# An expert stage on one Trainium2 core: every expert for every token, or sorted blocks of token and expert pairs

## The reference, cut to what matters

```python
logits = xf @ Wr + expert_bias                 # 4096 x 8
top_v, top_i = jax.lax.top_k(logits, 2)
probs = jax.nn.softmax(top_v, axis=-1)
rw = zeros_like(logits).at[arange(T)[:, None], top_i].set(probs)
gate = einsum('td,edf->tef', xf, Wg)           # 8 experts, 256 x 128
up = einsum('td,edf->tef', xf, Wu)
h = silu(gate) * up
eo = einsum('tef,efd->ted', h, Wd)             # 128 x 256
out = einsum('te,ted->td', rw, eo)
out = out + silu(xf @ Sg) * (xf @ Su) @ Sd     # the shared expert, 256 wide
x = layernorm(x + out)
```

## Time and profile before

| | us |
|---|---|
| median of 3 runs | 2544.12 (2532.03 to 2554.59) |
| profiled execution, span | 2541.9 |
| expert stage within it | 1048.7 to 1469.3 |

### The profile page before, as it was taken

How to read it: one execution, slowest core, us unless ns; L and a number is a source line. 1 busy time by engine, 2 the same in 40 slices (tenths; PEclk the granted TensorE clock), 3 DMA queues, 4 the chain that set the end, 5 groups by cost and what they waited for, 6 DMA issues and landing times. The chain is left out here.

```text
span 2541.9 us, 48920 instructions
## 1 busy us (share of the span) xinstructions
PE 2261.9 (89%) x17037; PEld 1586.3 (62%) x17037; DVE 1907.5 (75%) x4315; ACT 1507.2 (59%) x3369; POOL 1332.4 (52%) x1277
## 2 busy tenths in 40 slices
PE   5879999999999888799999979999878998999797
PEld 2555656565666555577787746666645776777555
DVE  5999999999999995367667458788845555566545
ACT  6778888888888864333333334554535667655522
POOL 2887979797878884233333224554553332321411
PEclk8979999999999998899999979999958999999898
DMA  6545444444544441100000234334120000000300
GB/s 208 165 139 170 151 152 160 142 164 137 167 139 163 137 146 54 50 30 1 1 1 1 51 80 77 73 56 69 36 78 2 21 23 19 18 19 19 113 15 9
DMA packets 139509, 206.87 MB, mean 81 GB/s; under 512 B 24481, under 2 KB 59426, under 8 KB 139138
## 3 DMA queue, kind: packets, MB, share of 16 engines
q1 hardware_dynamic: 137282, 200.86, 27.2%
q0 software_dynamic: 960, 2.62, 0.3%
q10 hardware_dynamic: 1024, 0.26, 0.1%
HBM read 161.42 MB, written 14.68 MB: 69 GB/s over the span
## 5 line engine op out<-in xcount | busy, mean ns | idle before, releaser
L534 POOL TENSOR_TENSOR ma_seen<-ma_state,ma_cs 128x1024 f32<-128x1024 f32 x256 | 602.7, 2366 | 179.8 <-DVE ma_state L1301 166.1
L1301 DVE TENSOR_TENSOR_SCAN ma_state<-ma_decay,ma_last,ma_drive 128x512 f32<-128x512 f32 x512 | 626.0, 1262 | 4.9 <-ACT ma_decay L1049 4.9
L1049 ACT ACTIVATE ma_decay<-ma_dt,ma_a_neg 128x512 f32<-128x512 f32 x512 | 338.7, 711 | 0.8 <-DVE ma_dt L1391 0.6
L1288 DVE TENSOR_TENSOR ma_drive<-ma_weight,ma_bs 128x512 f32<-128x512 f32 x512 | 325.6, 681 | 0.0
L770 PEld LDWEIGHTS ma_acc<-ident,ma_seen 128*128 128x128 f32 x2048 | 244.6, 147 | 114.8 <-POOL ma_seen L534 61.4
L770 PE MATMUL ma_acc<-ident,ma_seen 128*128 128x128 f32 x2048 | 273.7, 283 | 44.5 <-POOL ma_seen L534 44.4
L2453 DVE CUSTOM_DVE_ANT_0 sw_score<-sw_score,both_band 128x256 f32<-128x256 f32 (+1 forms) x512 | 197.2, 446 | 55.2 <-PE sw_score L2267 44.3
L2391 ACT ACTIVATE sw_prob<-sw_turned 128x512 f32<-128x512 f32 (+1 forms) x256 | 135.5, 581 | 172.6 <-PE sw_turned L2281 150.7
L104 POOL TENSOR_TENSOR moe_h_low<-both_V,light_wqkv 128x512 fp32r<-128x512 f32 x80 | 104.9, 1312 | 245.8 <-DVE light_wqkv L100 238.4
L2189 POOL TENSOR_SCALAR_AFFINE_SELECT sw_prob<-sw_prob 128x512 f32<-128x512 f32 x128 | 84.5, 660 | 202.5 <-ACT sw_prob L2391 202.5
L1913 DVE TENSOR_TENSOR both_V<-both_V,moe_up 128x512 f32<-128x512 f32 x80 | 55.0, 687 | 119.1 <-PE moe_up L1702 73.8
(11 more groups left out here) (596 smaller groups left out, 5715.9 us busy)
## 6 DMA issues: line engine op xcount, KB each, us to landing
ma_bs<-bc_rows SPq DMA_DIRECT2D x256, 256.0 KB, 3.3
ma_cs<-bc_rows SPq DMA_DIRECT2D x256, 256.0 KB, 3.3
ma_h<-kept_taps SPq DMA_DIRECT2D x28, 256.0 KB, 4.3
both_wide<-both_kh SPq DMA_DIRECT2D x28, 192.0 KB, 4.6
both_wide<-both_qh SPq DMA_DIRECT2D x20, 256.0 KB, 4.6
x_rows<-X SPq DMA_DIRECT2D x1, 4096.0 KB, 14.3
light_rows<-li_y SPq DMA_DIRECT2D x32, 128.0 KB, 1.7
out_dram<-li_o SPq DMA_DIRECT2D x32, 128.0 KB, 1.8
```

The source lines that it names most:

```text
L534: g.tensor_tensor(out=seen[n % RR][:, :, :], in0=state[n % SR][:, :, :], in1=each(cs[n % CR][:, :], 2), op=ALU.mult).then_inc(S["seen_full ...
L1049: a.activation(decay[s % DR][:, :], dt[:, m, :], ACT.Exp, scale=a_neg[:, m, k:k + 1]).then_inc(S["decay_done"], 1)
L1288: v.tensor_tensor(out=drive[mm][:, :], in0=weight[mm][:, :], in1=bs[n % CR][:, :], op=ALU.mult).then_inc(S["drive_done"], 1)
L1301: v.tensor_tensor_scan(state[n % SR][:, mm, :], decay[s % DR][:, :], drive[mm][:, :], last[:, k, m:m + 1], ALU.mult, ALU.add).then_inc(S[" ...
```

## The change

Only the expert stage is another (and the layout of two weights on the host). Tokens are handled per batch of 2048, and nothing is split in halves: all matmuls of the stage are plain f32, but for those of the lists, which are bf16 on whole numbers.

- TensorE opens with four groups turned and their logits. Then come the first 8 units of the shared expert alone (2 per group, 4 matmuls of 512 columns each, and per group 8 of 256 for down), with the other four groups' transposes and logits between them.
- Routing of a batch: VectorE takes the two best of 8 for 16 tiles at once. Two matmuls (L1700, L1701) count the tokens per expert, and a scan gives each (token, expert) pair its place: experts begin at multiples of 128, and there are 40 blocks of 128 places per batch (32 and one spare per expert). Four chunks of one-hot tiles (`list_chunk`) are multiplied on TensorE and give for each place its token's number (`listu`), and `experts_of` gives each block the offset of its expert's weights in a table (`etab`). For batch 0 this runs beside the front half of the shared expert, for batch 1 beside the first ten pairs.
- x is stored to DRAM as rows. GpSimd gathers the rows of a block by `listu` (`fetch`, 128 rows of 1 KB, two gathers per pair of blocks) into a ring of 16 pairs.
- 40 pairs of blocks: TensorE turns the rows (`turn_rows`), ScalarE copies them, TensorE loads the two offsets into registers and makes gate and up in one product of 256 columns per half of the inner dimension (`gates_ups`), ScalarE takes the silu, VectorE the product, TensorE turns it (`turn_hidden`), VectorE copies, TensorE makes down (`downs`), ScalarE copies and SyncE stores the rows to DRAM.
- GpSimd gathers, per tile of 128 tokens, the rows of its first and of its second expert (`collect`), and VectorE adds both to X with their probabilities and normalizes (`combine`, `normals`). Batch 0 is collected from pair 26 on, batch 1 beside the rear half of the shared expert, whose last 7 units follow the pairs together with the next layer's first products. Six tiles are left behind the last unit.

```diff
-UNITS = E + FS // P
-SLOTS_ALL = GROUPS * UNITS
+UNITS = FS // P
+SUNITS = GROUPS * UNITS
+FRONT = SUNITS // BATCH
+NT = SEQ // P
+NB = 2 * NT + E
+PAIRS_OF = NB // 2
+ALL_PAIRS = BATCH * PAIRS_OF
+LCH = 8
+CHUNKS_OF = 2 * NT // LCH
+XRING, ERING, CRING = 16, 3, 8
+LATE = 26
...
+            sp.dma_start(xrow[0].rearrange("(t p) d -> p t d", p=P), X[:, 0:NT, :]).then_inc(S["spill0"], 16)
...
+            for q in range(ALL_PAIRS):
+                b, k = divmod(q, PAIRS_OF)
...
+                sp.wait_ge(S["eo_copied"], q + 1)
+                sp.dma_start(erow[b][2 * k * P:2 * (k + 1) * P, :].rearrange("(c p) d -> p c d", p=P),
+                             eo[q % ERING].rearrange("p (c d) -> p c d", c=2)).then_inc(eo_out[q % ERING], 16)
...
+            def fetch(q):
+
+                b, k = divmod(q, PAIRS_OF)
+                if k == 0:
+                    pool.wait_ge(S["lists_full"], b + 1)
+                    pool.wait_ge(S[f"spill{b}"], 16)
+                since(pool, "xb_turned", q - XRING + 1)
+                for c in range(2):
+                    at = bass.IndirectOffsetOnAxis(ap=listu[b][:, 2 * k + c:2 * k + c + 1], axis=0)
+                    g.indirect_dma_start(out=x_ring[q % XRING][:, c, :], out_offset=None, in_=xrow[b], in_offset=at).then_inc(xg_in[q % XRING], 16)
+
+            def collect(m):
+
+                b, t = divmod(m, NT)
+                if t == 0:
+                    stored(pool, (b + 1) * PAIRS_OF)
+                since(pool, "combined", m - CRING + 1)
+                for s in range(2):
+                    at = bass.IndirectOffsetOnAxis(ap=posu[b][:, s, t:t + 1], axis=0)
+                    g.indirect_dma_start(out=c_ring[m % CRING][:, s, :], out_offset=None, in_=erow[b], in_offset=at).then_inc(cg_in[m % CRING], 16)
...
+            ahead = ALL_PAIRS - 4
+            for q in range(ahead):
+                fetch(q)
+            for m in range(TILES):
+                collect(m)
+                if m < ALL_PAIRS - ahead:
+                    fetch(ahead + m)
+                if m >= 5 and m % GT == 1:
+                    root(m // GT - 1)
...
+            def gates_ups(q):
+
+                b, k = divmod(q, PAIRS_OF)
+                if k == 0:
+                    pe.wait_ge(S["etab_full"], b + 1)
+                if q == 0:
+                    pe.wait_ge(S["gu_in"], 64)
+                pe.wait_ge(S["xb_copied"], q + 1)
+                if q < 2:
+                    pe.wait_ge(S["prod_done"], FRONT - 1 + q)
+                since(pe, "h_done", q - 1)
+                for c in range(2):
+                    where[q, c] = pe.value_load(etab[b][0:1, 2 * k + c:2 * k + c + 1], min_val=0, max_val=(E - 1) * D)
+                for c in range(2):
+                    for hh in range(DH):
+                        mine = table[:, hh * EW:(hh + 1) * EW][:, bass.ds(where[q, c], 2 * FE)]
+                        ins = t.matmul(pu[q % 2][:, c * D:(c + 1) * D], xbT[q % 2][:, c, hh, :], mine, start=(hh == 0), stop=(hh == DH - 1))
+                ins.then_inc(S["gu_done"], 1)
...
+            for q in range(ALL_PAIRS + 2):
+                if q < ALL_PAIRS:
+                    gates_ups(q)
+                if q == ALL_PAIRS:
+                    gate(FRONT)
+                    up(FRONT)
+                if 0 <= q - 1 < ALL_PAIRS:
+                    turn_hidden(q - 1)
+                if q + 2 < ALL_PAIRS:
+                    turn_rows(q + 2)
+                if 0 <= q - 2 < ALL_PAIRS:
+                    downs(q - 2)
+                middle(q)
...
+            for q in range(ALL_PAIRS + 2):
+                if 0 <= q - 1 < ALL_PAIRS:
+                    hidden_turned(q - 1)
+                if q < ALL_PAIRS:
+                    hidden(q)
+                if q == ALL_PAIRS:
+                    products(FRONT)
+                if q < 6 + CHUNKS_OF:
+                    route(1, q)
+                if 0 <= q - LATE < NT:
+                    collected(q - LATE)
```

More of the change, by code:

```diff
@@ L1501, in experts_block @@
[L1501 to L1506 removed]
+        ws, sd = A.sb("ws", [P, UNITS, 2, DH, P]), A.sb("sd", [P, UNITS, D])
+        table = T["V"][:, :, :, :].rearrange("p n h d -> p (n h d)")
@@ L1996 @@
+            normals(GROUPS - 1)
 CHUNKS = SEQ // P
```

864 lines of the change are left out of this document (485 added, 379 removed).

## The result

The changed kernel took 2404.97 us (median of five, 2399.32 to 2427.48) where the kernel before took 2543.12 on the same chip (five, 2532.03 to 2554.59): the ratio is 0.9473, with a 95% interval from 0.9427 to 0.952. The forecast was 2438 in a range from 2392 to 2500. The experiments then added something that one comparison could not show: how much the change brings is not the same on every chip that it ran on. In a later comparison the ratio was 0.95 again, and on another chip, with the same two programs, 0.9852.

A forecast was written before the change was run, and what follows sets the result against it. TensorE alone was taken to bound the expert stage. Its terms, 14 + 58 + 131 + 53 + 13 = 269 us, plus 38 for loads and 8 for hand-overs, made 315 instead of 420.6: forecast 2438 us, range 2392 to 2500.

The forecast's parts named there:

- What bounds it: Expert stage of 420.6 us: bound by TensorE alone, busy all of each 52 us stretch at granted clock 1.00.
- The term for the products: 40 pairs of blocks: six products of 0.43 us and six transposes, 3.2 us per pair, 128 us in all.
- The register loads: Before each pair on TensorE: two loads, 0.94 us per pair, 38 us; hand-overs 8 us more.
- I take the row nearest in kind: Price of a TensorE register load, taken from SyncE getting one DMA out every 0.47 us.
- rival 1: In the pairs, register loads are hidden wholly: stage 269 to 277 us, time 2392 to 2400 us; chance 0.2.
- A period of 3.3 speaks for rival 1: Sign in the pairs: a period of 3.3 us means hidden loads; the forecast expected 4.0 to 4.6 us.
- Its own case: Register loads before the pairs cost 0.2 to 1.1 us each, time 2408 to 2480 us; chance 0.58.
- The row it rested on: Evidence for hidden loads: TensorE's weight loads busy 40.97 of 52 us beside matmuls busy for all of them.
- Head and front: Stage's opening transposes and logits, 14 us; front half of the shared expert, 58 us.
- Rear, tail and close: After the pairs: 3 us to drain, rear half 53, tail on VectorE 12, closing the stage 1.
- Rival 2: GpSimd becomes the bound in the stage: gathers take 2.0 us, not 1.26; 66 us saved, 2478 us; chance 0.12.
- Rivals 3 and 4: Loads before pairs cost 2.5 us each, 2598 us, chance 0.06; clock falls to 1.2 GHz in pairs, 2520 us, chance 0.04.

The follow-up runs named there:

- third run of the same program: The changed kernel timed a third time, unaltered, on a further chip: 2407.08 us against 2538.34 for the kernel before, ratio 0.9499.

## Why the prediction was right, and where not

- *What bounds it.* TensorE bounded the stage before and bounds it now, on the quick kind of chip: busy 131 of 131 us through the pairs, granted clock 1.00. The term for the products held: 3.2 us per pair predicted, 3.24 measured.
- *The register loads.* The step that failed is "I take the row nearest in kind": 38 us for the loads and 8 for hand-overs. Neither is there; 46 predicted, under 2 measured (3.24 - 3.2, 40 times). What happened is rival 1's mechanism, given 0.2; its time of 2392 to 2400 was missed by the other terms. The prediction's own sign had it so: "A period of 3.3 speaks for rival 1". Its own case, loads of 0.2 to 1.1 us each and 2408 to 2480 us, did not come, and that 2405 lies in the range is in part luck (see the sum). The row it rested on, weight loads busy beside busy matmuls, was the better sign than the row for a price: the question was not what a load costs but whether TensorE has matmuls in hand meanwhile. With 3.2 us in hand two loads of 0.64 disappear: 3.25 us a step with them and without them on the same chip. With eight the step is 6.77 us, and they do not. The Trainium skill ("TensorE: Matmul & The Clock Gate", table at the head) gives TensorE a queue of 64. The traces agree: on the quick chip a pair's first load starts at 1181.50, 3.0 us ahead of its first product at 1184.46. The 200 ns per register of the Trainium skill ("Runtime: NRT & Kernel Launch", section Instruction fetch mechanics) are for loads from HBM; a load from SBUF took 0.30 us here.
- *Head and front.* 73.1 us against 72. The head took 4.7 more, with TensorE busy all through it and a granted clock of 0.59 from 1050 to 1070, and the front 3.6 less. (The front's terms as listed add up to nearly 59 and not 58.)
- *Rear, tail and close.* 88.9 against 69: 20 us too few. Three things. The rear is 7 longer, with a wait of 3.94 for VectorE at its end. The tail is 18.6 and not 12: the sentence "then 32 x 1.26 = 40 us fit beside the 53 of the rear half" counted the gathers and not what stands between them in GpSimd's order, the power that waited 16 us. And "1 to close the stage as before" was wrong by 6.6: a drain behind 144 gathers takes 8.85 us, and one more in the middle shortens it to 3.78.
- *GpSimd as the bound.* Rival 2's price was 2.0 us per gather. Most kept 1.25. Three gathers that ran beside VectorE's one-hot work for the list took 1.58, 1.64 and 1.94 us and not 0.95, too few to count: the mean of the 80 is 982 ns. That is the direction of the shared port in the Trainium skill ("SBUF — State Buffer", section Who interferes with whom); that the port is the cause was not tried. GpSimd's first 72 gathers left in one row, so it did not wait for TensorE to turn rows, as the prediction's full ring had it.
- *Rivals 3 and 4.* No load costs 1.8 us, and the clock did not fall in the pairs on the quick kind. On the slow kind it does, in the stretches in which TensorE had work for 13 of 30 us (0.71 and 0.85 above).
- *Sum.* The pairs were given 44.4 us too many and everything else 21 too few, which makes the stage 23 shorter than forecast: two errors that partly cancel. The medians differ by 138 and not by 129, and what is left over is behind the stage. That part does the same work in both kernels, and its length varies from execution to execution. The next stage by stretch (TensorE alone: stretch, us, busy, clock, DMA share, GB/s), its last part in the profiled execution of the changed kernel and then in the third run of the same program:
```profile
1674.00:1773.10 99.10, 90.61 (x882) 0.61 0.02 5
```
```profile
1674.00:1744.10 70.10, 55.39 (x811) 0.99 0.01 3
```
The stage, begun within 1 us of the same time in both (1341.67 and 1340.88), ends 29 us sooner where the granted clock is 0.99 and not 0.61. In the profiled execution of before it was 0.76 over the last 84 us, and its executions lie 22 us apart. A gain of this size stands above it; one of 7 us does not.
- *What no step had.* That the gain depends on where it is run. On the slow kind the changed kernel took 2494, just inside the range's end of 2500 and for none of the reasons that set that end, which is luck; nothing in the trace of before, with its few gathers, spoke of it.

## To carry to other kernels

Ask of a scalar load or any work of a sequencer first whether the engine behind it has enough queued, and only then what it costs: two loads were free under 3.2 us of matmuls, eight were not, and by the estimate above a third might already show. When work is taken off TensorE and put on gathers, write down GpSimd's whole order, since anything that waits in it holds up every gather behind it, and count the drain at the end. Long rows of gathers are worth breaking up where a run shows late signals, and a deeper ring, which lets rows grow, can lose more than it wins. And measure such a change on more than one chip: here the same two programs stood 5.3 and 5.0% apart in two comparisons, and 1.5% on another chip.

## What the runs showed of the hardware

- GpSimd's drain at a block's end took 0.30 us with no gathers since the last drain, 3.78 to 3.97 with 32 and 8.85 to 9.05 with 144. One behind 112, in the middle, took 15.3, of which 9.2 came after the last of the gathers still in hand: the number of gathers alone doesn't set it.
- A load of one number from SBUF into a register of TensorE takes 0.30 us, and with the register instructions behind it 0.64 when exposed. Two per pair cost nothing under 3.2 us of matmuls.
- On three of four chips signals between engines came up to 30 us late while GpSimd issued gathers without a pause; on the fourth, and in the first comparison, never, though a row of 72 went out there. Gathers in fours and twos cost TensorE next to nothing on such a chip (VectorE up to 1.8 us late beside fours, 0.04 beside twos). What the late signals wait for is not settled: the profile names no releaser, and whether it is the gathers' descriptors, the signals of their landing or something else of these chips was not tried. The loss goes with the row's length: rows of 20 gathers (25 us) cost TensorE 20 us, rows of 28 and 30 cost 30 to 34. Breaking one row up into fours and twos took its loss away; rows of eight with 1.2 us between still cost 13.6 us in a rear.
- A rear with earlier gathers and a second drain ends the stage 11 us sooner after TensorE's last matmul, at the price of 17 us before it on a slow chip. Whether it makes the kernel faster on a quick chip is open: it ran on the slow kind only.
